# Calling a Newton step on VectorE earlier and shifting the last gathers in a two-layer gated transformer kernel

## What is computed

```python
def _layernorm(x, axis=-1, eps=1e-05):
    m = jnp.mean(x, axis=axis, keepdims=True)
    v = jnp.var(x, axis=axis, keepdims=True)
    return (x - m) / jnp.sqrt(v + eps)
...
x = x + jnp.tanh(g_xattn[0]) * _L0_xattn_ref(_layernorm(x, axis=-1), ctx_1024, ctx_1024, ...)
x = x + jnp.tanh(g_ffn[0]) * _L0_ffn_ref(_layernorm(x, axis=-1), ...)
x = x + jnp.tanh(g_xattn[1]) * _L1_xattn_ref(_layernorm(x, axis=-1), ctx_1024, ctx_1024, ...)
x = x + jnp.tanh(g_ffn[1]) * _L1_ffn_ref(_layernorm(x, axis=-1), ...)
```

## Time and profile before

| | us |
|---|---|
| median of 3 runs | 938.26 |
| lowest and highest | 935.92, 938.75 |
| the profiled execution | 938.75 |
| its span, first to last instruction | 936.9 |

### The profile page before, as it was taken

How to read it: one execution, slowest core, us unless ns; L and a number is a source line. 1 busy time by engine, 2 the same in 40 slices (tenths; PEclk the granted TensorE clock), 3 DMA queues, 4 the chain that set the end, 5 groups by cost and what they waited for, 6 DMA issues and landing times.

```text
span 936.9 us, 20428 instructions
## 1 busy us (share of the span) xinstructions
PE 787.5 (84%) x6554; PEld 621.6 (66%) x6554; DVE 689.5 (74%) x1980; ACT 609.5 (65%) x2582; POOL 546.7 (58%) x798
## 2 busy tenths in 40 slices
PE   3658999889975499999777779788888889999996
PEld 1346666666753499998455546556756668888885
DVE  5648899999988344445889799998897676666664
ACT  2549988889863254534876778889996444444442
POOL 4254668888586202030657887574414867777775
PEclk9979999999997699999988899999999999999998
DMA  7978977756338343224428267445200000000000
GB/s 177 217 201 234 234 236 194 164 135 135 82 95 283 131 148 83 84 75 112 100 64 156 76 131 154 123 113 135 69 13 24 23 23 23 24 23 13 9 4 23
DMA packets 85139, 101.68 MB, mean 109 GB/s; under 512 B 8448, under 2 KB 70853, under 8 KB 84360
## 3 DMA queue, kind: packets, MB, share of 16 engines
q1 hardware_dynamic: 80936, 92.13, 38.4%
q0 software_dynamic: 4096, 8.25, 3.5%
HBM read 63.32 MB, written 45.99 MB: 117 GB/s over the span
## 4 chain that ended last, share of the span: by engine, by line
PE 38%; DVE 24%; ACT 14%; issue 9%; POOL 8%; DMA 5%; SPq 1%; POOLq 0%; DVEq 0%; ACTq 0%
ACT exp L854 11%; PE psum L697 7%; DVE shift L1039 5%; PE psum L737 5%; PE psum L739 5%; PE psum L738 5%; DVE exp_T L1049 2%; DVE exp_T L1051 2%; PE psum L685 2%; DVE ln_stats L1021 2%; PE psum L686 2%; PE psum L687 2%; DMA scratch_q<-parts 2%; POOL scratch_xe L1566 2%; PE psum L580 2%
## 5 line engine op out<-in xcount | busy, mean ns | idle before, releaser
L854 ACT ACTIVATE exp<-psum,shift 128x120 f32<-128x120 f32 x1024 | 366.7, 437 | 76.4 <-DVE shift L1039 76.0
L854 ACT ACTIVATION_READ_ACCUMULATOR exp<-psum,shift 128x1 f32 x1024 | 274.3, 282 | 0.0
L1039 DVE TENSOR_REDUCE shift<-psum 128x4 f32<-128x480 f32 x256 | 165.6, 647 | 38.6 <-PE psum L558 37.6
L567 PE MATMUL psum<-ident,exp 128*120 128x128 f32 x1024 | 163.3, 284 | 32.9 <-DVE exp_T L1051 18.8
L1420 DVE SCALAR_TENSOR_TENSOR q_operand<-psum,comb,q_operand 128x256 f32<-128x256 f32 x256 | 111.6, 479 | 73.6 <-ACT q_operand L986 73.6
L1657 POOL TENSOR_TENSOR q_operand<-q_operand 128x512 f32<-128x512 f32 x96 | 126.4, 1317 | 58.4 <-DVE q_operand L1420 53.5
L567 PEld LDWEIGHTS psum<-ident,exp 128*120 128x120 f32 x1024 | 118.6, 142 | 52.0 <-DVE exp_T L1051 24.7
L986 ACT ACTIVATE q_operand<-psum 128x512 f32<-128x512 f32 x128 | 76.2, 599 | 114.7 <-PE psum L739 114.7
L1585 POOL DMA_INDIRECT got_rows<-scratch_y,slot_get x64 | 67.0, 1047 | 123.6 <-DMA scratch_y<-y_rows 107.1
L555 PE MATMUL psum<-neg_rows,const_bf 128*128 128x480 bf16 x256 | 98.4, 384 | 39.9 <-ACT exp L854 31.6
L558 PE MATMUL psum<-k_operand,q_operand 128*128 128x240 bf16 x512 | 97.8, 274 | 0.0
(11 more groups left out here) (175 smaller groups left out, 1671.5 us busy)
## 6 DMA issues: line engine op xcount, KB each, us to landing
k_operand<-scratch_k SPq DMA_DIRECT2D x32, 360.0 KB, 6.4
q_operand<-scratch_q SPq DMA_DIRECT2D x30, 384.0 KB, 6.5
scratch_q<-parts SPq DMA_DIRECT2D x15, 384.0 KB
scratch_k<-parts SPq DMA_DIRECT2D x14, 360.0 KB, 4.4
scratch_xe<-in_zero_rows SPq DMA_DIRECT2D x8, 512.0 KB, 7.7
scratch_y<-in_zero_rows SPq DMA_DIRECT2D x8, 512.0 KB
scratch_q<-parts SPq DMA_DIRECT2D x15, 256.0 KB
scratch_k<-parts SPq DMA_DIRECT2D x14, 240.0 KB, 4.6
```

What stands on the lines that cost most here:

```text
L567: ins = pe.transpose(ps[0:S2, T_BANKS[G % 2], u * S:(u + 1) * S], atts[l].expS[:, G % RING_E, u, :], ident[:, :])
L854: ins = act.activation(atts[l].expS[:, G % RING_E, u, :], ps[:, S_BANKS[G % 3], u * S2:(u + 1) * S2], ACT.Exp, bias=atts[l].shift[:, i % 2 ...
L1039: dve.tensor_reduce(atts[l].shift[:, i % 2, 4 * r:4 * r + 4], ps[:, S_BANKS[G % 3], 0:4 * S2].rearrange("p (h k) -> p h k", h=4), AX_X, AL ...
```

## The change

It has three parts.

1. `roots` is called at the slot `power` instead of at the slot `norm` for chunks 1, 2 and 3 of layer 1's attention and for chunks 6 and 7 of layer 0's experts. The normalisation stays where it was. For the three chunks of layer 1, `power` is the same slot as `stat` (6, 15 and 24), and `norm` is slot 9, 17 and 26. For chunk 6, `power` is slot 124 and `norm` slot 127. For chunk 7 (slots 140 and 143), no instruction of DVE lies between the two, so that its order stays the same.
2. For the half chunk among the expert jobs, `roots` is called right behind its statistics (`ADD_NEXT`) instead of two jobs later (`NORM_NEXT`).
3. `bring_slot`: the gathers of chunk 5 begin at slot 30 instead of 29, those of chunk 6 at 45 instead of 37, and those of chunk 7 at 60 instead of 52.

```diff
@@ def bring_slot(i):
-    return {8: 0, 9: 7, 10: 9, 11: 11}[i] if c == 2 else {3: 13, 4: 21, 5: 29, 6: 37, 7: 52}[c] + 2 * b
+    return {8: 0, 9: 7, 10: 9, 11: 11}[i] if c == 2 else {3: 13, 4: 21, 5: 30, 6: 45, 7: 60}[c] + 2 * b
@@ vector_program, behind(l, s)
                 if l == 1 and P in ON_DVE1:
+                    if o == at["power"]:
+                        roots(0, C)
                     if o == at["norm"]:
-                        roots(0, C)
                         normalise_rows(0, C, P)
@@
+                if l == 0 and j >= ON_DVE and o == post_at(l, j)["power"]:
+                    roots(1, j)
                 if l == 0 and j >= ON_DVE and o == post_at(l, j)["norm"]:
-                    roots(1, j)
                     normalise_rows(1, j, j)
@@ vector_program, experts0()
                     stat_rows(0, HALVED, 1, 1, 1)
+                    roots(0, HALVED, 1)
                 if n == NORM_NEXT:
-                    roots(0, HALVED, 1)
                     normalise_rows(0, HALVED, 1, 1)
```

## The result

The changed kernel takes 950.56 us (median of four runs, 949.31 to 952.72) against 938.28 for the kernel before in the same comparison: a ratio of 1.0139, with a 95% interval of 1.0113 to 1.0164. By the ratio that is +13.0 us (10.6 to 15.4), by the medians +12.3, where +7.3 was forecast. The sign was right. The median itself lies within the forecast's range of 940.5 to 951, close to its top; the ratio, applied to the kernel before, gives 951.3 and lies just above it. The profiled execution took 948.68 us, with a span of 946.9, so the two traces differ by 10.0 us. That is less than the medians do, and the trace can only account for those 10.0.

What follows compares the result with a forecast made beforehand. No engine was taken as full over the whole program (PE 84%, DVE 74% busy); the bound depends on the stage. Terms 4.2 + 0 + 1.4 + 1.5 + 0.7 - 0.5 = +7.3 on 938.75 gave 946 us, range 940.5 to 951.

Steps and rivals of the forecast that it cites:

- Place one: Roots of chunk 6, layer 0: DVE waits 4.28 us for POOL's power; +4.2 us in all (3.0 to 5.5).
- The half chunk: Roots of the half chunk among the experts: the 1.3 us wait is covered, as DVE waits for PE anyway; 0.
- Chunks 1, 2 and 3: Roots in layer 1's attention: DVE waits 1.54, 1.54 and 2.91 us for POOL's power, costing +1.4, +1.5 and +0.7 us.
- Up to 1.4 late: Behind chunk 3's wait in layer 1, POOL's power for chunk 4 begins up to 1.4 us late; +0.7 us taken.
- The gathers: Later gathers of chunks 5 to 7 in layer 1's attention: -0.5 us together (-4 to +3).
- just in time: Slice 30's second gather is issued at 597.4 and lands at 600.3, for an add_y at 600.57.
- What DVE wins elsewhere it would wait away again: At the later gathers: DVE's gains in other places would be lost waiting for them; no separate size.
- No fixed sign: Shifted gathers move where add_y meets POOL's instructions; each such meeting loses DVE 1 to 2 us, net sign open.
- Only place one counts: Rival: layer 1's moved roots cost nothing and one gather less saves 1.3 us; 941.65 us, chance 0.16.
- The clock falls as well: Rival: stalls leave PE idle, its clock falls to 0.50 and transposes slow; up to 951.5 us, chance 0.14.
- The gathers win: Rival: moved gathers let slow add_y run at their median and win more than the waits cost; 930 us, chance 0.05.
- The move does nothing: Rival: POOL would be ahead of DVE, so moved roots cost no wait; 938.3 us, chance 0.03.

Runs made afterwards that it cites:

- e_powfirst: Kernel before with only layer 0 chunk 6's roots moved, and POOL's power of chunk 6 put ahead of slots of chunk 5: 962.49 us, ratio 1.0040.
- e_gathers_b: Kernel before with only the gathers' new slots (chunk 5 at 30, chunk 6 at 45, chunk 7 at 60), second run: 940.96 us, ratio 1.0047.
- e_g7: Kernel before with only chunk 7's gathers moved, from slot 52 to 60: 940.84 us, ratio 1.0037.
- e_g6: Kernel before with only chunk 6's gathers moved, from slot 37 to 45: 964.14 us, ratio 1.0058.
- before: The kernel before, unchanged, in the first comparison: 938.28 us.
- after: The changed kernel, all three parts against the kernel before, in the first comparison: 950.56 us, ratio 1.0139.
- r_before: The kernel before, unchanged, run again under another label against itself: 936.23 us, ratio 0.9997.
- r_after: The changed kernel, all three parts, run again against the kernel before: 948.28 us, ratio 1.0132.
- e_mid: Kernel before with the gathers of chunks 6 and 7 four slots later (41 and 56): 933.46 us, ratio 0.9974.
- e_best: Kernel before with chunk 5's gathers at slot 30 and those of chunks 6 and 7 at 41 and 56: 931.44 us, ratio 0.9956.
- e_roots_mid: Changed kernel with the gathers of chunks 6 and 7 at 41 and 56 instead of 45 and 60: 939.56 us, ratio 1.0045 to the kernel before.
- e_l1roots_b: Kernel before with only the roots of chunks 1, 2 and 3 of layer 1 moved, second run: 958.60 us, ratio 1.0004.

## Why the prediction was right, and where it was wrong

**The waits of the roots: right in place and size.** All five stand where they were forecast, to within 0.15 us. This was a reading of two rows for each wait: when DVE goes on, and when POOL's power ends.

**Place one: right, as far as shown.** Forecast +4.2; +3.8 and +4.9 measured alone, and 4.3 at the first expert matmul by the traces. Its terms stand in the trace too, counted from the end of `positions` at 270.24 and 269.02: chunk 6's normalisation starts at 277.79 instead of 275.31, which is 3.7 late (forecast 4.0). The clock fell: 0.50 from 273 to 281, with four transposes in 1.08 to 1.11 us, where the kernel before had 1.00 and 0.62 to 0.65. With it DVE's weights for POOL (L1199) are 5.35 late, and chunk 7's normalisation, where the wait of 0.83 us for the scatters is gone, 4.6. `e_powfirst` shows that the stall is POOL's order. It does not show that the program gets the time back without the stall.

**The half chunk: right**, 0, with PE as the last to arrive behind it.

**Chunks 1, 2 and 3: right in sign, and not settled in size.** Forecast 1.4 + 1.5 + 0.7 = 3.6. By the traces of the changed kernel they are 1.3, 2.0 and nothing. Alone they cost 0.4 and 1.5 us in the sets where the kernel before took 959 us; all roots less place one's 4.2 leave 4.8 us where it took 936 (3.5 by the medians). "Up to 1.4 late" for POOL's power of chunk 4 was wrong: DVE's gap took up the whole 2.91.

**The gathers: the failed step.** The term was -0.5 us, and they cost +4.4 (2.9 to 5.8). What failed is the overlap, "the gathers are just in time": DVE stood 2.3 us for the landing at slice 30, and the place of slice 30 alone lost 3.7. Three things went into it.

- "Just in time". The queue in front of the gather was worked out well: 21.3 us from POOL's power to the issue, against 21.7 in `e_gathers_b` (597.4 and 597.48). But "lands after 2.9 us" took the median of the row for a gather that falls into a stretch full of other transfers; it took 4.7. The row had 6.5 as its maximum, and that end was not carried into the term.
- "What DVE wins elsewhere it would wait away again" was right, and should have been priced: `e_g7` waits 4.9 us at this one instruction. A term whose own working says that everything is waited away can't be negative. What it could do was cost.
- "No fixed sign" for the meetings: they cost here too. 3.19 us stood at slice 29, where two of POOL's instructions come back to back beside an `add_y`; the kernel before had 1.43 and 1.24 there, so 0.9 of it is new. The L1156 of slice 30 adds another 0.9.

What was wrong the other way is chunk 5: up to -1.3 was allowed, and -2.0 came (-3.4 to -0.6, so -1.3 isn't excluded). Why chunk 6's gathers alone cost 5.6 us stays open, and with it how the 4.4 divide among the chunks.

**The rivals.** *Only place one counts* is out: the whole is 12.3. *The clock falls as well* gives about the measured time (951.5), which is chance, since it does not come about by its mechanism. The clock falls at place one, which the forecast has already. The granted clock of the whole went from 0.949 to 0.946, it stays at 1.00 behind the stall of chunk 1 (461 to 467 us), and the transposes behind the stall of chunk 2 are no slower than they were at the earlier trace rows:

```profile
487.03 1.09 PE L501 MATMUL psum<-ident,xn_rows 128*128 128x128 f32 x4 [2.04 <-DVE xn_rows L1182]
```

*The gathers win* is out for this change, but with half the shift they do win, by 4.1 us. *The move does nothing* is out.

## What to carry to other kernels

A wait that is moved can be priced from two rows, the asking engine's next start and the giving engine's end; whether it reaches the end of the program depends on the next gap on the asking engine, and only a run tells. A fetch that is issued later should be held against its worst landing, in the traffic of the stretch that it moves into, not against the median: here four slots later gained 2.4 us and eight lost 3.5 and more. Where the working says "just in time", the range belongs on the side of the loss.

## What the runs showed of the hardware

- One instruction of DVE can stand over two of POOL's that follow each other: L1156 took 3.19 us beside two of 1.27 and 1.16 us, in the changed kernel and in the runs of the gathers alone. And `add_y` isn't the only one: in `e_g6` a copy (L1062) took 1.83 us where the median is 0.23, and an operation on 4 columns (L1141) 2.00 where it is 0.17. The Trainium skill, "SBUF — State Buffer", section Who interferes with whom, says that copies and operations with a scalar can also take the port pair that VectorE shares with GpSimd, where their operands meet its conditions, and then contend for it. By that rule, the trace agrees.
- A gather by POOL landed in 2.7 us (median) and in 4.7 us while the SP queue moved 640 KB beside it. The traces of nine runs (`before`, `after`, `r_before`, `r_after`, `e_gathers_b`, `e_g7`, `e_mid`, `e_best`, `e_roots_mid`) show the landing of 202 gathers behind 446 us. Where the DMA engines were busy under 30% in the 2.5 us after the issue, it took 2.6 us (median; 2.5 to 3.8), where over 80%, 5.0 (3.0 to 10.5). In the kernel before, the one issued at 487.14 took 2.65 us at a DMA share of 0.20, and the one at 510.69 took 6.48 at 1.00. The Trainium skill, "DMA: Bandwidth & Descriptors", section Latency and other measured facts, says that an access to HBM takes 0.2 us on average and 2 us at high load. The difference of 2.0 us here is of that size; that the load is its cause was not tried by itself.
- The same kernel took 936 us in some sets and 959 in others, once of each kind on one chip. All the roots together cost less in the latter (4.5 us against 9.0, by the medians 5.3 against 7.7). Counted from slot 0 of the first attention, the trace of `e_l1roots_b` (956.0 us) is 0.9 us ahead of that of `r_before` (935.0) at slot 90, 13.1 behind at the first expert matmul, 19.8 at slot 60 of the second attention and 20.5 at the end, far more than its moved waits. So the longer time comes in two stretches, and what makes it stays open.
